# A state-space kernel on one core: the Silu of xc waits for one sum in place of sixteen, and nine steps of the schedule move

## The reference

```python
xz = u @ in_proj_w.T
xh, z = (xz[:, :d_inner], xz[:, d_inner:])
xp = jnp.pad(xh, ((D_CONV - 1, 0), (0, 0)))
conv = conv_b
for k in range(D_CONV):
    conv = conv + xp[k:k + L] * conv_w[:, k]
xc = jax.nn.silu(conv)
dbc = xc @ x_proj_w.T
dt = dbc[:, :dt_rank]
Bm = dbc[:, dt_rank:dt_rank + D_STATE]
Cm = dbc[:, dt_rank + D_STATE:]
delta = jax.nn.softplus(dt @ dt_proj_w.T + dt_proj_b)
A = -jnp.exp(A_log)

def step(h, t):
    d, b, c, xt = t
    h = h * jnp.exp(d[:, None] * A) + (d * xt)[:, None] * b[None, :]
    return (h, h @ c)
...
y = ys + xc * D
y = y * jax.nn.silu(z)
...
y = y @ out_proj_w.T
p = y @ proj_w.T + proj_b
mu = jnp.mean(p, axis=-1, keepdims=True)
var = jnp.mean(jnp.square(p - mu), axis=-1, keepdims=True)
p = (p - mu) * jax.lax.rsqrt(var + LN_EPS) * ln_g + ln_b
p = jax.nn.silu(p)
out = jnp.transpose(p.reshape(B, H, W, C), (0, 3, 1, 2))
return out + x
```

## Time and profile before

| | |
|---|---|
| time, median of 3 runs | 13710.69 us (13707.44 to 13711.41) |
| time of the profiled execution | 13714.89 us |
| its span | 13713.1 us |
| TensorE matmul | 12193.3 us busy (89%) |
| VectorE | 10302.8 us busy (75%) |
| ScalarE | 7816.4 us busy (57%) |
| GpSimd | 7304.6 us busy (53%) |
| mean granted clock of TensorE | 0.93 |

### The profile page before, as it was taken

The page is one execution under the profiler, slowest core; times in us unless marked ns, Lnnn a source line. Parts: engine busy times, 40 slices in busy tenths (PEclk is TensorE's granted clock), DMA queues, the critical chain, the costliest instruction groups (busy, mean ns, idle before and its releaser), DMA issues.

```text
span 13713.1 us, 161052 instructions
## 1 busy us (share of the span) xinstructions
PE 12193.3 (89%) x34109; PEld 4484.8 (33%) x34285; DVE 10302.8 (75%) x13211; ACT 7816.4 (57%) x12823; POOL 7304.6 (53%) x5412
## 2 busy tenths in 40 slices
PE   4989999898999988888888888888888888888888
PEld 1333333333333333333333333333333333333333
DVE  6454545545454368988898898889888889889888
ACT  1333333333333357766677677777777777766776
POOL 6030311303030047777777777777777777777777
PEclk9989999898999989999999999999999999999999
DMA  2010010101000023333333333333333333333333
GB/s 54 2 26 9 20 27 2 26 2 26 9 20 2 2 104 138 138 138 138 138 138 138 138 138 138 138 138 138 139 137 140 142 139 137 140 141 138 138 138 138
DMA packets 372433, 1297.68 MB, mean 95 GB/s; under 512 B 177904, under 2 KB 177904, under 8 KB 231792
## 3 DMA queue, kind: packets, MB, share of 16 engines
q1 hardware_dynamic: 372336, 1296.81, 25.5%
HBM read 1246.07 MB, written 50.56 MB: 95 GB/s over the span
## 4 chain that ended last, share of the span: by engine, by line
DVE 17%; issue 16%; PE 16%; ACT 13%; DVEq 1%; ACTq 0%; POOL 0%; DMA 0%; POOLq 0%; SPq 0%
DVE bbank L905 9%; PE ybank L1140 6%; ACT da L1035 5%; DVE h L919 5%; PE bbank L1130 2%; PE pbank L1121 2%; PE ubank L1100 1%; PE vbank L1098 1%; ACT L976 1%; DVE yb L893 1%; PE ybank L1138 1%; DVE qn L897 1%; PE pbank L1116 1%; ACT so L1009 1%; ACT xc L968 1%
## 5 line engine op out<-in xcount | busy, mean ns | idle before, releaser
L838 POOL TENSOR_TENSOR pr<-h,cc 128x512 f32<-128x512 f32 x4110 | 5187.9, 1268 | 2088.0 <-DVE h L919 1912.6
L919 DVE TENSOR_TENSOR_SCAN h<-da,h,bbank 128x512 f32<-128x512 f32 x4110 | 5201.7, 1266 | 1.1 <-ACT da L1035 1.1
L1140 PE MATMUL ybank<-pr,m_small 128*128 128x512 f32 x8214 | 4415.9, 625 | 0.0
L905 DVE TENSOR_TENSOR bbank<-bbank,du 128x512 f32<-128x512 f32 x4111 | 2784.7, 677 | 899.1 <-PE bbank L1130 894.7
L1035 ACT ACTIVATE da<-dl,a 128x512 f32<-128x512 f32 x4114 | 2737.2, 713 | 18.5 <-DVE dl L886 2.4
L432 ACT ACTIVATE prob<-st 128x512 f32<-128x512 f32 x2048 | 1222.7, 597 | 2576.4 <-PE st L564 2576.4
L307 DVE TENSOR_REDUCE mpart<-s 128x1 f32<-128x512 f32 x2048 | 1322.5, 686 | 1091.1 <-PE s L530 1082.8
L564 PE MATMUL st<-qf,kf 65*128 (+1 forms) x4096 | 2122.6, 621 | 5.9 <-ACT qf L436 5.9
L1140 PEld LDWEIGHTS ybank<-pr,m_small 128*128 128x128 f32 x8214 | 1659.3, 204 | 969.4 <-issue 623.6
L1130 PE MATMUL bbank<-bcs,selb 96*128 96x512 bf16 x4113 | 1693.4, 412 | 230.8 <-DVE h L919 209.2
L240 POOL TENSOR_TENSOR rowsum<-xin 128x1024 f32<-128x1024 f32 x64 | 153.9, 2404 | 2997.0 <-PE vb L597 2907.9
(11 more groups left out here) (153 smaller groups left out, 11753.8 us busy)
## 6 DMA issues: line engine op xcount, KB each, us to landing
cc<-c_rows SPq DMA_DIRECT2D x1032, 1024.0 KB, 8.0
upw<-up SPq DMA_DIRECT2D x260, 256.0 KB, 9.4
xin<-x SPq DMA_DIRECT2D x128, 512.0 KB, 6.8
out<-ot SPq DMA_DIRECT2D x256, 128.0 KB, 2.3
zw<-zn_tokens SPq DMA_DIRECT2D x780, 32.0 KB, 9.7
c_rows<-crows SPq DMA_DIRECT2D x258, 32.0 KB, 1.7
zn_tokens<-znb SPq DMA_DIRECT2D x64, 128.0 KB, 2.0
a_small<-small SPq DMA_DIRECT2D x1, 1331.0 KB, 5.8
```

Source lines behind the costliest of these rows:

```text
L838: pool.tensor_tensor(pr[:, n % 8, :], h[:, n, :], cc[par][:, n, :], ALU.mult).then_inc(prod_done, 1)
L905: dve.tensor_tensor(bbank[n % 4][:, :], bbank[n % 4][:, :], du[par][:, :], ALU.mult)\
L919: dve.tensor_tensor_scan(h[:, n, :], da[:, n % 8, :], bbank[n % 4][:, :], h[:, n, TB - 1:TB], ALU.mult, ALU.add).then_inc(scan_done, 1)
L1140: pe.matmul(ybank[:, :], w("ident"), pr[:, n % 8, :], start=False, stop=(n == S - 1))\
```

## The change

The Silu of xc waits for `sum_mm` at `(tau - 2) * S + 1`, which is the first sum of tile tau - 2, instead of `(tau - 1) * S`, which is all of its sums. On GpSimd `cv`, `l2` and `du` go to steps 7, 8 and 12, and the residual to 4. On VectorE `dl` goes to step 11. On ScalarE the two later casts of B go to steps 7 and 10, Square to 8, Ln and Exp to 11. On TensorE the two corrections of B go to steps 6 and 9. The matmuls `pc` and `var` and the products `yb` and `qn` stay where they were.

```diff
         @block.gpsimd
             def prep(n, tau, par):
-                if n == 6:
+                if n == 7:
 ...
                     pool.tensor_tensor(cv[:, :], ed[:, :], ev[:, :], ALU.subtract).then_inc(cv_done, 1)
-                if n == 7:
+                if n == 8:
 ...
                     pool.tensor_tensor(l2[:, :], lv[:, :], cv[:, :], ALU.subtract).then_inc(l2_done, 1)
-                if n == 11:
+                if n == 12:
 ...
                     pool.tensor_tensor(du[par][:, :], dl[par][:, :], xc[par][:, :], ALU.mult).then_inc(du_done, 1)
             def post(n, g, s, k):
-                if n == 6:
+                if n == 4:
                     residual(g, 1 - s, k)
 ...
         @block.vector
             def prep(n, tau, par, first):
-                if n == 10:
+                if n == 11:
 ...
         @block.scalar
                     if not first:
-                        act.wait_ge(sum_mm, (tau - 1) * S)
+                        act.wait_ge(sum_mm, (tau - 2) * S + 1)
                         act.wait_ge(du_done, tau - 1)
 ...
-                if n == 6:
+                if n == 7:
                     act.wait_ge(rest_mm, tau + 1)
                     act.copy(bcs[par][0:64, :], ubank[0:64, :]).then_inc(mid_done, 1)
-                if n == 8:
+                if n == 10:
                     act.wait_ge(last_mm, tau + 1)
                     act.copy(bcs[par][0:32, :], ubank[0:32, :]).then_inc(bcs_done, 1)
 ...
-                if n == 6:
+                if n == 8:
                     act.wait_ge(pc_mm, g + 1)
                     act.wait_ge(var_mm, g)
                     act.activation(sq, pbank[0:64, :], ACT.Square, bias=pbc[:, :]).then_inc(sq_done, 1)
-                if n == 9:
+                if n == 11:
                     act.wait_ge(var_mm, g + 1)
 ...
         @block.tensor
-                if n == 5:
+                if n == 6:
                     pe.wait_ge(hi_done, tau + 1)
 ...
-                if n == 7:
+                if n == 9:
                     pe.wait_ge(mid_done, tau + 1)
```

## The result

The changed kernel takes 12704.92 us (median of 4 runs, 12702.59 to 12708.35), against 13709.07 us before in the same comparison. The ratio is 0.9268, 95% interval 0.9252 to 0.9284: 1004 us less. The forecast was 12720.

What follows compares the result with a forecast made beforehand. TensorE's lateness, which makes VectorE wait, was taken as the bound: 256 tiles of 3.87 us are 991 us, so 13714.9 - 991 - 4.2 = 12720 us, range 12680 to 13010, chance 0.66.

Steps and rivals of the forecast that it cites:

- What bounds: TensorE late behind ScalarE's wait for the sixteenth sum, VectorE waiting at L905: 3.87 us of a 34.13 us tile.
- The floor: VectorE's own pace where nothing is late: 13 x 1.78 + 7.12 = 30.26 us a tile.
- The Silu's wait: On ScalarE, the load starts at 2.85 us, xc is done at 4.8; TensorE, ready at 6.2, doesn't wait.
- The walk: TensorE's order through a tile after the Silu's change: spreads 8 to 11 have margins of 1.3 us or more.
- The new wait for Square: On TensorE before var, step 8: some 1.2 us a tile; taken at nothing, upper bound 0.5 us.
- The moves at nothing: Moved steps on ScalarE, TensorE, GpSimd and VectorE: priced at nothing, bounds 0 and 0.5 us a tile.
- The clock: TensorE keeps full clock, the longest hole being 1.2 us before var; otherwise VectorE waits 0.7 to 2.4 us.
- Rival 1: TensorE's clock still falls in most tiles, 0.7 to 2.4 us each: 13030 us, bounds 12900 and 13330; chance 0.18.
- Rivals 2 to 4: New wait at Square or du, 12850 (0.07); Silu not freed, 13700 (0.05); TensorE's clock lost for good, 14910 (0.04).

Runs made afterwards that it cites:

- 15 sums: The changed kernel with the Silu waiting for 15 of the old tile's 16 sums, `(tau - 1) * S - 1`: 12836.6 us, ratio 0.9363 to the kernel before.

## Why the prediction was right, point by point

- What bounds: the holes on TensorE, made by ScalarE's lateness behind the sixteenth sum, with the low clock behind them, were the whole loss. The Silu's wait alone shows it: it brings all of the gain.
- The floor: 30.26 us a tile forecast, 30.21 measured. The plain step is 1.77 us on the changed trace, where I took 1.78; 0.05 x 256 = 13 us is most of the 15 us between forecast and result.
- The Silu's wait: the load starts 0.16 us after L1091 in one kind of tile and earlier in the other (below). TensorE doesn't wait for xc.
- The walk: with L1091's end put at 2.78 as there, the tile shown has L1098 at 6.15 (6.2 forecast), Abs at 9.27 (9.2), and TensorE ready for var at 16.68 (16.6). It holds for this kind of tile; the forecast knew only one kind.
- The new wait for Square: 1.2 us forecast in each tile, 1.11 measured in every second one and 0.17 in the others.
- The moves at nothing: right in the sum and for the casts' own cost. But the walk gave them a part in curing L1109's wait, which they weren't needed for: without them that wait shrinks to 1.1 us in every second tile, and the kernel is as fast. Taken alone, and without Square's, they are worth 644 us.
- The clock: full clock was right in the main, and in part by luck, since kernels one small step away lose it. The argument for it was weaker than it looked. I took 1.2 us before Square as the longest hole and didn't see the two waits at steps 13 and 14, 1.12 and 1.18 us in every second tile. In the changed kernel a stretch with TensorE busy 1.25 of 3.40 us keeps 1.00; with Square back at 6 one with 1.52 of 3.40 is followed by 0.50. And in the changed kernel itself the same two waits, 1.12 and 1.18 us, stand once before full clock and once before a low stretch. So neither busy time nor the length of a hole, as read from these rows, says when the clock falls.
- Rival 1 did come about, in three near relatives of the changed kernel, at about 0.5 us a tile instead of 0.7 to 2.4. With Square back the clock falls in 122 of 163 tiles, and VectorE waits 0.5 us for each, where the term had 0.7. With 15 sums and with Square at 10 it falls in 26 and 34, so the terms' fall in most tiles is what was wrong there. In the changed kernel it falls in 9. Behind rival 1 stood the Trainium skill (TensorE: Matmul & The Clock Gate, "A second HAM failure mode: psum-queue depth-cycling"); by that rule the clock should fall in both kernels that have two short waits for a free bank in each tile. The kernel with Square back agrees, with 122 falls; the changed kernel, whose waits are of like length in every second tile, agrees only in 9 of 165 tiles.
- Rivals 2 to 4 did not occur: VectorE's idle time before its products is 9.5 us in all, the old wait was the sums', and the clock isn't lost for good.

Open: three kernels that differ in their holes and in their clock (0.953 and 0.968) end within 3 us of each other, at 12834 to 12837. They get there by different sums: one has many low stretches with a short wait behind each and no other lateness of the spreads, the two others have few, with long waits, and short waits in tiles without one. No run here says that the meeting is more than chance. Also open is why equal waits are followed by a low stretch in some tiles and not in others.

## What to carry to other kernels

A wait on a counter is worth reading as an index: which read of the buffer is the last, and which count proves it. Here 15 of 16 sums had nothing to do with xc, and one line held 7.3% of the time. Moving steps apart treats the same lateness at its effect; test the parts alone, since a bundle may hold moves that add nothing beside a better one, and one (Square) that takes away what the others bring. When one engine sets the pace, look where the others gather their idle time, because on TensorE that place can cost its clock; what then pays is taking operations off the pacing engine.

## What the runs showed of the hardware that was not expected

- More work on TensorE made two kernels faster: 13346.8 against 13709.0 us, and 12692.1 against 12833.6, with 3.4 and 1.7 us more matmuls a tile, and neither has a stretch under full clock from 7000 to 12000 us.
- Two waits of 1.12 and 1.18 us on TensorE, the same to 0.01 us, were followed by full clock in one tile of the changed kernel and by a low stretch in another; there are nine such stretches in 165 tiles.
- The table load in front of the Silu starts after the convolution in one tile and ahead of it in the next. In the next tile of the changed kernel, ScalarE:

```profile
9045.15 1.28 ACT L968 ACT_TABLE_LOAD   x1
9046.81 0.69 ACT L968 ACTIVATE xc<-vbank,m_small 128x512 f32<-128x512 f32 x1 [0.38 <-PE vbank L1091]
```

The load lies under the convolution there (L1091 starts at 9045.76), and xc starts 1.05 us after L1091 does. In the tile shown above it starts 9018.06 - 9015.59 = 2.47 us after it. The two tiles of a loop turn alternate so, 83 and 82 times. Why only one of the two bodies does it was not tried.
